# A head's output turned, divided and turned back by VectorE in 32x32 blocks, and laid out for Wo through DRAM

## The reference

```python
# attention(xn), first half (the change is here): 16 heads of 16 columns, per batch
qk = (ln1(x) @ Wqk_t) split in heads;  v = (ln1(x) @ Wv_t) split in heads
logits = (2*qk@qk.T - q2[:, None] - q2[None, :]) / sqrt(16) * tau_t
out = softmax(logits) @ v                      # [2048, 16] per head
x = x + (out of all heads side by side) @ Wo_t * gamma1
# second half: the same between channels: 8 blocks of 32 channels, attention over [32, 32]
x = x + channel_diffusion(ln2(x)) * gamma2
# experts(xn): top-1 of 8 experts, gate * (relu(xn @ W1[e] + b1[e]) @ W2[e] + b2[e])
```

## Time and profile before

| what | us |
|---|---|
| median of 3 runs (lowest, highest) | 1493.56 (1493.15, 1494.26) |
| the profiled execution: its own time | 1493.66 |
| its span | 1491.8 |
| stage 1 | 0 to 116.5 |
| attention loop, plain pairs 0 to 2 | 116.5 to 314.9 |
| attention loop, expert pairs 3 to 15 | 314.9 to 1356.9 |
| between last values and first work of the tail | 1356.9 to 1366.6 |
| tail | 1366.6 to 1491.8 |
| PE busy / ACT busy / DVE busy / POOL busy | 1410.5 / 1074.1 / 384.5 / 168.6 |

### The profile page before, as it was taken

How to read it: one execution, slowest core, us unless ns; L and a number is a source line. 1 busy time by engine, 2 the same in 40 slices (tenths; PEclk the granted TensorE clock), 3 DMA queues, 4 the chain that set the end, 5 groups by cost and what they waited for, 6 DMA issues and landing times. The chain is left out here.

```text
span 1491.8 us, 27128 instructions
## 1 busy us (share of the span) xinstructions
PE 1410.5 (95%) x9233; PEld 684.1 (46%) x9233; DVE 384.5 (26%) x977; ACT 1074.1 (72%) x1191; POOL 168.6 (11%) x186
## 2 busy tenths in 40 slices
PE   6988999999999999999999999999999999996988
PEld 4652222234444444444444444444444444444877
DVE  6872100011111111111111111111111111112986
ACT  4657999987777777777777777777777777773221
POOL 5210710000000000000000000000000000000870
PEclk9998999999999999999999999999999999998999
DMA  4686532724544536254454544544526345520323
GB/s 162 240 232 207 137 74 54 206 33 127 136 106 145 122 105 146 83 150 116 103 163 100 158 108 108 153 106 137 129 82 163 90 132 135 128 92 33 110 89 112
DMA packets 119863, 186.96 MB, mean 125 GB/s; under 512 B 20208, under 2 KB 89520, under 8 KB 116624
## 3 DMA queue, kind: packets, MB, share of 16 engines
q1 hardware_dynamic: 114880, 172.92, 42.7%
q0 software_dynamic: 4944, 13.51, 3.0%
HBM read 150.43 MB, written 31.75 MB: 122 GB/s over the span
## 5 line engine op out<-in xcount | busy, mean ns | idle before, releaser
L909 ACT ACTIVATE shared<-ps 128x1024 f32<-128x1024 f32 x1024 | 982.1, 1023 | 265.2 <-PE ps L1070 263.3
L1085 PE MATMUL ps<-shared,work 128*17 128x512 f32 x4096 | 500.3, 597 | 0.4
L1070 PE MATMUL ps<-mov,stat 52*128 52x512 f32 x2048 | 421.8, 464 | 39.0 <-ACT shared L909 25.3
L1070 PEld LDWEIGHTS ps<-mov,stat 52*128 52x128 f32 x2048 | 166.6, 185 | 408.7 <-ACT shared L909 386.0
L980 DVE TENSOR_SCALAR work<-ps,work 128x128 f32<-128x128 f32 x312 | 109.5, 351 | 576.2 <-PE ps L1142 561.3
L1085 PEld LDWEIGHTS ps<-shared,work 128*17 128x17 f32 x4096 | 89.4, 96 | 219.9 <-issue 202.7
L1142 PE MATMUL ps<-work,XNW 128*128 128x128 f32 x1248 | 180.7, 287 | 0.0
L1142 PEld LDWEIGHTS ps<-work,XNW 128*128 128x128 f32 x1248 | 151.0, 191 | 56.9 <-issue 56.9
L1124 PE MATMUL ps<-XNW,work 128*128 128x256 f32 x624 | 161.8, 382 | 0.0
L865 POOL DMA_DIRECT2D y_slots<-work x39 | 21.6, 553 | 840.3 <-DVE work L972 840.3
L1124 PEld LDWEIGHTS ps<-XNW,work 128*128 128x128 f32 x624 | 106.4, 191 | 12.8 <-issue 4.8
(11 more groups left out here) (172 smaller groups left out, 697.4 us busy)
## 6 DMA issues: line engine op xcount, KB each, us to landing
XNW<-in_L_ffn_W_dram SPq DMA_DIRECT2D x78, 1024.0 KB, 7.1
stat<-q_parts SPq DMA_DIRECT2D x192, 128.0 KB
mov<-q_parts SPq DMA_DIRECT2D x192, 64.0 KB
xg<-in_L_attn_x_dram SPq DMA_DIRECT2D x16, 512.0 KB, 4.7
q_parts<-XNW SPq DMA_DIRECT2D x16, 512.0 KB, 5.6
x_slots<-work SPq DMA_DIRECT2D x1, 4992.0 KB, 17.7
early<-x_slots SPq DMA_DIRECT2D x39, 128.0 KB, 2.2
early<-in_L_ffn_b_dram SPq DMA_DIRECT2D x39, 128.0 KB, 9.5
```

Source lines behind the costliest of these rows:

```text
L909: nc.scalar.activation(probs[:, s % DEEP, half * 1024:(half + 1) * 1024], ps[:, 2 * half:2 * half + 2].rearrange("p a b -> p (a b)"), ACT. ...
L1070: last = nc.tensor.matmul(ps[:, 2 * half + r], stat[rows, hh, m * P:(m + 1) * P], mov[rows, hh, half * 512:(half + 1) * 512], start=True, ...
L1085: last = nc.tensor.matmul(ps[32 * j:32 * j + VW, AV], Vh[:, hh, m], probs[:, s % DEEP, j * 512:(j + 1) * 512], start=(m == 0), stop=(m == ...
```

## The change

A head's output is now handled by DVE alone. DVE transposes AV in 32x32 blocks straight from PSUM (`turn_o`): block b of a partition group of 32 then has tokens on the partitions and the 17 rows as its first 17 columns. It takes 16 reciprocals per partition, multiplies in place and transposes again in 32x32 blocks (`norm_o`), so the 16 channels are on partitions 32*j to 32*j+15 again, each with 512 tokens. POOL stores these four pieces of [16, 512] to a new DRAM tensor `a_turned` [channels, tokens] (`store_o`, four DMAs per head, 128 in all). PE's unit "o" is gone, and so are the transposes `turn_a` of the tail and ACT's copies `take_at`. AT is now the memory of V, [channels, tokens], loaded from `a_turned`: batch 0 by one DMA of SP at the end of stage 2, batch 1 by four DMAs of SP in stage 3.

Moved with it: `values` of a new head waits for `o_turned`, the first transpose. The turn of the last head, the last two `store_y`, the wait for `y_stored` (now ahead of the first indirect fetch, and in ACT's stream ahead of a later copy) and the load of XN groups 4 and 5 move behind the meeting of the engines into stage 3. `make_x1` waits for its own part of XN only. DVE's last `norm_o` stands behind the clearing of the banks.

```diff
+        def store_o(i, hh):
+            head = 2 * i + hh
+            nc.gpsimd.wait_ge(o_ready, head + 1)
+            for j in range(NCHUNK):
+                nc.gpsimd.dma_start(a_turned[bass.ds(head * DH, DH), j * 512:(j + 1) * 512],
+                                    o_cols[32 * j:32 * j + DH]).then_inc(o_stored, 16)
...
+        def turn_o(i, hh):
+            head = 2 * i + hh
+            at_least(nc.vector, o_ready, head)
+            nc.vector.wait_ge(av_done, TB * (head + 1))
+            nc.vector.transpose(o_rows, ps[:, AV]).then_inc(o_turned, 1)
+        def norm_o(i, hh):
+            head = 2 * i + hh
+            o = o_rows.rearrange("p (b e) -> p b e", e=32)
+            nc.vector.wait_ge(o_turned, head + 1)
+            nc.vector.reciprocal(rec, o[:, :, DH]).then_inc(rec_ready, 1)
+            nc.vector.wait_ge(rec_ready, head + 1)
+            nc.vector.tensor_tensor(o[:, :, 0:DH], o[:, :, 0:DH], rec.unsqueeze(2).broadcast_to([P, TB, DH]),
+                                    ALU.mult).then_inc(o_scaled, 1)
+            nc.vector.wait_ge(o_scaled, head + 1)
+            at_least(nc.vector, o_stored, 16 * NCHUNK * head)
+            nc.vector.transpose(o_cols, o_rows).then_inc(o_ready, 1)
...
 # SP, end of stage 2
-                for tt, groups in ((0, (0, 1, 6, 7)), (1, (2, 3)), (2, (4, 5))):
-                    sp.wait_ge(y_taken, 3 * (PAIRS - 1 - FIRST) + tt + 1)
-                    for G in groups:
-                        at = slice(G * GT, (G + 1) * GT)
-                        sp.dma_start(XN[:, at], xn_rows[:, at]).then_inc(xn_back, 16)
+                sp.wait_ge(o_stored, 16 * NCHUNK * H)
+                sp.wait_ge(v_copied, H)
+                sp.dma_start(AT[:, 0], a_turned[0:D].rearrange("(c p) n -> p c n", p=P)).then_inc(at_loaded[0], 16)
+                load_xn(0)
+                load_xn(1)
...
 # POOL, expert pairs and end of stage 2
                 with pool.Fori(FIRST, PAIRS - 1) as i:
                     store_y(i, 0)
                     copy_v(i + 1, 0)
+                    store_o(i, 0)
                     store_y(i, 1)
                     store_y(i, 2)
                     copy_v(i + 1, 1)
-                for tt in range(3):
-                    store_y(PAIRS - 1, tt)
-                for tt in range(3):
-                    pool.wait_ge(y_stored[tt], 16 * (PAIRS - FIRST))
+                    store_o(i, 1)
+                store_y(PAIRS - 1, 0)
+                store_o(PAIRS - 1, 0)
...
 # stage 3: SP, POOL, DVE, PE
+                load_xn(2)
+                sp.wait_ge(o_stored, 16 * NCHUNK * NB * H)
+                sp.wait_ge(v_copied, NB * H)
+                for j in range(NCHUNK):
+                    at = slice(j * 512, (j + 1) * 512)
+                    sp.dma_start(AT[:, 1, :, at], a_turned[D:2 * D, at].rearrange("(c p) n -> p c n", p=P)
+                                 ).then_inc(at_loaded[1], 16)
...
+                for tt in (1, 2):
+                    store_y(PAIRS - 1, tt)
+                store_o(PAIRS - 1, 1)
                 for G in range(GROUPS):
                     rstd(G, G % 2)
+                    if G == 0:
+                        for tt in range(3):
+                            pool.wait_ge(y_stored[tt], 16 * (PAIRS - FIRST))
...
+                turn_o(PAIRS - 1, 1)
+                dve.wait_ge(o_turned, NB * H)
                 nc.vector.memset(ps[:, 4:6], 0.0).then_inc(gram_cleared, 1)
+                norm_o(PAIRS - 1, 1)
...
-                dve.wait_ge(xn_back, 16 * GROUPS)
                 make_x1(0, 0)
...
                 def project(G, par):
-                    pe.wait_ge(ring3_taken, use_a(G) + 2)
+                    b, at = G // GB, (G % GB) * GN
+                    pe.wait_ge(at_loaded[b], 16 if b == 0 else 16 * NCHUNK)
```

More of the change, by code:

```diff
@@ L737, in build, with ring_base @@
         scattered = sem("scattered")
-        def ring_base(i, experts):
-            if isinstance(i, int) and i == 0:
-                return 0
-            if not experts:
-                return 2 * i - 1
-            return 2 * FIRST - 1 + 32 * (i - FIRST)
-        def plain_plan(i):
-            steps = [[] for _ in range(STEPS)]
-            if not (isinstance(i, int) and i == 0):
-                steps[1].append(("o", 1, -1))
-            steps[TB + 1].append(("o", 0, 0))
-            return steps
+        def ring_base(i):
+            return 30 * (i - FIRST)
         def expert_plan():
@@ L775, in use_numbers, with bank, store_y, load_xn @@
             return table
-        def bank(i, k):
-            first = 0 if isinstance(i, int) and i == 0 else 1
-            return RING + (first + k) % 2
+        def bank(k):
+            return RING + k % 2
         x_again = [sem("x_again0"), sem("x_again1")]
-        xn_back = sem("xn_back")
+        xn_back = [sem(f"xn_back{k}") for k in range(3)]
+        at_loaded = [sem("at_loaded0"), sem("at_loaded1")]
+        HOMES = ((0, 1, 6, 7), (2, 3), (4, 5))
+        def store_o(i, hh):
[4 more added lines that the diff above has]
+                                    o_cols[32 * j:32 * j + DH]).then_inc(o_stored, 16)
+        def store_y(i, tt):
+            n = 3 * (i - FIRST) + tt
+            nc.gpsimd.wait_ge(y_taken, n + 1)
+            nc.gpsimd.dma_start(y_slots[bass.ds(n * P, P), :], ysb[:, tt]).then_inc(y_stored[tt], 16)
+        def load_xn(tt):
+            nc.sync.wait_ge(y_taken, 3 * (PAIRS - 1 - FIRST) + tt + 1)
+            for G in HOMES[tt]:
+                at = slice(G * GT, (G + 1) * GT)
+                nc.sync.dma_start(XN[:, at], xn_rows[:, at]).then_inc(xn_back[tt], 16)
+        def turn_o(i, hh):
[14 more added lines that the diff above has]
+            nc.vector.transpose(o_cols, o_rows).then_inc(o_ready, 1)
         with nc.Block() as block:
@@ L860, in copy_v @@
                     fill_v(i, hh)
-                def store_y(i, tt):
-                    n = 3 * (i - FIRST) + tt
-                    pool.wait_ge(y_taken, n + 1)
-                    pool.dma_start(y_slots[bass.ds(n * P, P), :], ysb[:, tt]).then_inc(y_stored[tt], 16)
                 pool.wait_ge(routed, 1)
@@ L877, in _ @@
                 copy_v(1, 1)
+                store_o(0, 1)
                 for i in range(2, FIRST + 1):
-                    copy_v(i, 0)
-                    copy_v(i, 1)
+                    for hh in range(2):
+                        copy_v(i, hh)
+                        store_o(i - 1, hh)
                 with pool.Fori(FIRST, PAIRS - 1) as i:
@@ L1282, in _ @@
             def _(act):
-                def take_at(G, par):
-                    for c in range(KC):
-                        act.wait_ge(ring3_ready, use_a(G) + c + 1)
-                        if c == 0:
-                            at_least(act, wo_ready, 2 * (G - 1))
-                        nc.scalar.copy(AT[:, par, c], ps[:, c]).then_inc(ring3_taken, 1)
                 def take_a2(G, par):
@@ L1368, in make_x1 @@
                 def make_x1(G, par):
+                    for tt in range(3):
+                        if G in HOMES[tt]:
+                            dve.wait_ge(xn_back[tt], 16 * len(HOMES[tt]))
                     for k in range(2):
@@ L1616, in _ @@
                 corner(0)
-                turn_a(GROUPS - 1)
                 product_t(0)
```

156 lines of the change are left out of this document (54 added, 102 removed).

## The result

| | median of the runs, us | profiled run, us | its span | granted clock |
|---|---|---|---|---|
| before | 1493.91 (1493.15 to 1494.60) | 1493.66 | 1491.8 | 0.989 |
| after | 1479.08 (1476.98 to 1480.64) | 1478.41 | 1476.7 | 0.987 |

The ratio is 0.990, 95% interval 0.9888 to 0.9912. The change saves 14.8 us.

What follows compares the result with a forecast made beforehand. ACT was taken to bound plain pairs, PE expert pairs, POOL's drain the meeting and DVE the middle of the tail. 1493.7 - 9.6 (loop) - 12.2 (meeting) - 4.4 (tail) = 1467.5 us, range 1461 to 1478.

Steps and rivals of the forecast that it cites:

- plain pairs, 5 turns: Loop, plain pairs: taking out PE's turns of five heads saves 2.8 us.
- expert pairs, 13 turns in rounds 0 and 8: Loop, expert pairs: turns cost 0.09 us in round 0 and 0.43 in round 8; 13 pairs save 6.8 us.
- DVE's and POOL's new work in the loop: Loop: DVE's transposes, reciprocals and products and POOL's four stores per head lie in slack; cost 0.
- the meeting: Between attention and tail: DVE's second addition of group 0 comes 12.2 us earlier (11.0 to 13.4).
- the first part of the tail: Middle of the tail: DVE falls out of step with POOL's `add_x` and leads by 4.4 us (0 to 6.0).
- the second part: Tail from POOL's last inverse root on: nothing changes, 0 us.
- rival 3: Loop: a DVE float32 transpose costs many times a copy and delays `values`; at 4 us, 1515; chance 0.04.
- PE comes last: At the meeting: POOL's drain and SP's load end near 1331, PE at 1356.9 + 0.1.
- rival 2: Meeting: `a_turned` returns from DRAM late, or another late comer: 1476 to 1480; 0.13, shared with a transpose up to 2 us.
- rival 4: PE's clock falls in the loop or the tail begins wholly cold: 1469 to 1470; chance 0.25 together with rival 1.
- From there on all is as before: Tail behind POOL's last inverse root: the 4.4 us lead is kept to the end, nothing else changes.
- Rival 1: Tail: DVE stays in step with `add_x`, POOL sets the pace, no lead: 1472; chance 0.25 together with rival 4.

Runs made afterwards that it cites:

- again: The kernel after, run once more unchanged: 1478.70 us.
- before_meet: The kernel before, with only POOL's last two stores of y and its wait for `y_stored` moved behind the meeting of the engines: 1486.61 us, ratio 0.9951.
- after_nomeet: The kernel after, with POOL's last stores of y and the wait for them put back at the end of stage 2; on another chip, ratio 0.9894.
- fill4: The kernel after, with four idle PE transposes of the identity added in round 0 of each expert pair: 1473.31 us, ratio 0.9863.
- before_none0: The kernel before, without PE's turn of the head's output in round 0 of expert pairs; on another chip, ratio 1.0025.
- fill_r6: The kernel after, with four idle PE transposes in round 6 of each expert pair, none in round 0; on another chip, ratio 0.9838.
- fill4_mid_x: The kernel after with idle PE transposes in round 0 and mid-tail, and POOL's addition of x for group 5 behind the last four fetches: 1468.90 us, ratio 0.9833.
- fill4_late8: The kernel after with four idle PE transposes in round 0, and POOL's last eight fetches moved behind group 7; on another chip, ratio 0.9832.
- before_short0: The kernel before, with one of the four PE transposes of the turn kept in round 0; on another chip, 1528.78 us, ratio 1.0021.
- addmid: The kernel after, with POOL's addition of x in the tail placed between the second and third fetch of a group: 1478.43 us, ratio 0.9894.
- mid: The kernel after, with 20 idle PE transposes ahead of group 6's Gram product and 16 ahead of the product with Wo_c: 1477.17 us, ratio 0.9887.
- fill4_mid: The kernel after, with idle PE transposes both in round 0 of expert pairs and at two places mid-tail: 1471.62 us, ratio 0.9859.

## Why the prediction was wrong

Term by term, in us of the span:

| step | forecast | measured |
|---|---|---|
| plain pairs, 5 turns | -2.8 | -2.7 (160.98 to 158.24 from head 0 to head 5) |
| expert pairs, 13 turns in rounds 0 and 8 | -6.8 | -5.7 (80.25 to 79.82 us in pairs 4 to 14) |
| PE's clock in round 0 | 0 | +6.6 (4 x 1.65) |
| DVE's and POOL's new work in the loop | 0 | 0, as far as any row shows |
| the meeting | -12.2 | -13.3 (-11.6 in `again`) |
| the first part of the tail | -4.4 | -3.7 |
| the second part | 0 | +3.8 |
| sum | -26.2 | -15.0; span -15.1 |

- The transposes: right. 0.717 us against the 0.69 taken; rival 3 needed 3.3.
- The turns that go: right in kind. Round 0 saved nothing (0.09 forecast), round 8 the 0.43.
- "PE comes last" at the meeting: right. PE projected at the full clock in this profile, not halfway as I had taken; that is the 1.1 us in its favour, and it is luck, since in six of eleven profiles it didn't. before_meet and after_nomeet show that 5 to 7 of the 13 us are POOL's last wait and its drain. The rest I put down to the turns and ACT's copies that are gone; no run takes those out alone.
- The way of `a_turned`: right, nobody waited (rival 2 is out).
- The step that failed in the loop is the size of rival 4, "PE's clock falls in the loop ... 1469 to 1470, inside the range". I had seen that the turn of round 0 was hidden and took its removal for free. But hidden work on PE was also what kept PE busy: its idle time in the round went from 0.4 to 1.0 us, and the clock fell in 3 or 4 pairs of 13. That cost 6.6 us where rival 4 allowed 1.5 to 2.5 for the loop and the tail's start together. fill4, before_none0 and fill_r6 show it from three sides.
- The step that failed in the tail is the sentence "From there on all is as before". The lead came, 3.7 of 4.4 us. Behind it POOL's addition met DVE's four small products, which stand on PE's chain (2.1 us, shown by fill4_mid_x), and PE, idle longer, did two products of that chain at the low clock (2.8 us, the difference between runs at either level). Before, the addition met DVE's L1393 instead, and the low clock and that hold ran side by side. Without either loss B is 53.5 us (58.4 - 2.1 - 2.8, and fill4_mid_x has it); the kernel before had 54.6, so the two together cost it 1.1.
- Rival 1 came out with a similar number to a part of this and is wrong as a mechanism: DVE did fall out of step, and POOL's chain is not the bound (fill4_late8). At its last inverse root POOL was idle for 2.05 us, where it had 5.98.

With both causes removed the kernel takes 1468.9 us, 1.4 over the forecast. That is closer than the terms were: by the profiles the loop gave 1.2 us less than forecast, the meeting 0.6 less and A 0.8 less, and B gave 1.2 that the forecast did not have. The terms were right in kind, and what was missing was what the freed time sets off.

What stays open: which pairs get the low clock, and in which executions. Idle times of 0.43 us (before), 0.57 (fill4) and 0.75 (the profiled execution of before_short0) in round 0 gave none of 13, 0.90 gave 1, 1.0 gave 3, 4 or, in before_none0, 7. But pair 3, which follows a plain pair, was slow in the kernel after and in addmid at 0.28 + 0.41 = 0.69 us, so the idle time of the round is not a limit on one side of which nothing falls; and pairs with the same two idle times fell on both sides. And why the products behind the wait of 2.8 us were slow in mid and fast in fill4_mid isn't shown; the two kernels differ ahead of the tail alone.

## What to carry to other kernels

Before you take hidden work off a busy TensorE, look at the gaps that it leaves, and set the durations of the same matmuls in all repetitions side by side: here a stretch that was 1.7 times as long in some of them was the clock. When a stage gets ahead, follow it into the next one, and name which instruction of another engine its additions and waits will now meet. And look at what ends last where engines meet before you look at their work: half of this gain was POOL's last wait, put a few lines later.

## What the runs showed of the hardware

- A 32x32-block transpose on DVE of 128x512 float32 takes 717 ns from PSUM and 712 ns from SBUF, hardly more than a copy (691).
- TensorE's granted clock falls to its lower level within a loop in which PE is busy for 77 of 80 us, in some of the rounds in which it was idle for 0.60 and 0.41 us just before (0.28 and 0.41 at the least); the 16 products behind it then take 3.3 to 3.6 us instead of 1.91. Four idle transposes in that gap (0.16 and 0.41 left) gave no such round in four profiles of 13 pairs.
- Even a DVE product of 32x64 elements, 0.216 us by itself, takes 2.34 us beside one POOL addition of 128x1024.
- POOL's drain at the end of the attention loop took 3.3, 3.7, 5.9 and 7.1 us in four kernels (after_nomeet, after, before, before_meet). In after and before_meet it was over before the other engines were done and cost nothing.
